# Row maxima over pairs of PSUM banks in six of sixteen attention units, and the transposed maxima in the scores' ring

## The reference

```python
xn = layernorm(x)                                   # x is (4, 512, 512)
q  = (xn @ wq).reshape(B, T, 32, 16)                # 32 heads of 16
k, v = xn @ wk, xn @ wv                             # one key and value head for all
scores = einsum('bqhd,bkd->bhqk', q, k) / 4
probs  = softmax(where(causal, scores, -inf))
s = einsum('bhqk,bkd->bqhd', probs, v).reshape(B, T, C) @ wo
g = silu(linear8bit(linear8bit(xn, W1, b1), W2, b2))  # rows rounded to int8 steps, outlier columns apart
out = x + s * g
```

## Time and profile before

| what | us |
|---|---|
| median of three runs | 789.14 |
| the three runs | 788.95, 789.14, 1225.57 |
| the profiled execution | 788.52 |
| its span, first to last instruction | 786.8 |
| attention, about | 82 to 400 |

### The profile page before, as it was taken

The page is one execution under the profiler, slowest core; times in us unless marked ns, Lnnn a source line. Parts: engine busy times, 40 slices in busy tenths (PEclk is TensorE's granted clock), DMA queues, the critical chain, the costliest instruction groups (busy, mean ns, idle before and its releaser), DMA issues. The chain is left out here.

```text
span 786.8 us, 11983 instructions
## 1 busy us (share of the span) xinstructions
PE 752.1 (96%) x4133; PEld 567.0 (72%) x4133; DVE 651.5 (83%) x1116; ACT 396.0 (50%) x671; POOL 273.6 (35%) x349
## 2 busy tenths in 40 slices
PE   5999899999999999999999999999997999999995
PEld 4877575556666677666568878878886888888884
DVE  7988989999989999987447668597859998599957
ACT  4454066676777677667824445355554333132212
POOL 7213135555555555555442112122100000027404
PEclk9999689999999999999999999999999999999998
DMA  7431302332333332233455677646334678427982
GB/s 261 157 108 54 78 21 70 86 83 76 91 91 105 89 83 84 83 83 122 135 192 185 166 237 197 202 105 161 88 62 131 240 241 255 157 87 245 332 278 107
DMA packets 93772, 110.71 MB, mean 141 GB/s; under 512 B 43136, under 2 KB 50320, under 8 KB 92176
## 3 DMA queue, kind: packets, MB, share of 16 engines
q1 hardware_dynamic: 93712, 109.95, 45.8%
HBM read 56.43 MB, written 40.37 MB: 123 GB/s over the span
## 5 line engine op out<-in xcount | busy, mean ns | idle before, releaser
L933 DVE TENSOR_REDUCE rowmax<-ps 128x2 f32<-128x512 f32 (+3 forms) x384 | 210.7, 590 | 20.3 <-PE ps L1010 18.7
L854 ACT ACTIVATE probs<-ps 128x512 f32<-128x512 f32 (+1 forms) x352 | 175.3, 557 | 72.0 <-PE ps L1023 70.3
L1010 PE MATMUL ps<-km,stack 128*128 128x256 f32 (+3 forms) x512 | 150.2, 347 | 2.6 <-PEq L195 1.9
L1023 PE MATMUL ps<-stack,ks 128*128 128x512 f32 (+1 forms) x352 | 132.8, 387 | 2.7 <-ACT probs L854 2.7
L1010 PEld LDWEIGHTS ps<-km,stack 128*128 128x128 f32 (+1 forms) x512 | 95.1, 199 | 43.1 <-DVE rowmax L933 23.5
L836 POOL TENSOR_SCALAR_AFFINE_SELECT probs<-probs 128x512 f32<-128x512 f32 x128 | 81.0, 641 | 78.9 <-ACT probs L854 77.3
L1880 PE MATMUL ps<-big_h 128*128 128x512 f32 x256 | 100.0, 390 | 2.0 <-DVE big_l L1696 1.6
L1881 PE MATMUL ps<-big_l,big_h 128*128 128x512 f32 x256 | 99.6, 389 | 0.0
L1882 PE MATMUL ps<-big_h,big_l 128*128 128x512 f32 x256 | 99.6, 389 | 0.0
L1036 PE MATMUL ps<-probs,vones 128*32 128x512 f32 (+3 forms) x1024 | 82.2, 439 | 0.2 <-POOL probs L836 0.2
L1023 PEld LDWEIGHTS ps<-stack,ks 128*128 128x128 f32 x352 | 67.4, 192 | 11.7 <-ACT probs L854 6.2
(11 more groups left out here) (227 smaller groups left out, 1370.0 us busy)
## 6 DMA issues: line engine op xcount, KB each, us to landing
stack<-big_h SPq DMA_DIRECT2D x128, 64.0 KB, 2.0
h_scratch<-hs SPq DMA_DIRECT2D x7, 1024.0 KB, 4.7
hload<-h_scratch SPq DMA_DIRECT2D x14, 512.0 KB, 5.2
xn_scratch<-xa SPq DMA_DIRECT2D x4, 1024.0 KB, 4.4
stack<-big_l SPq DMA_DIRECT2D x64, 64.0 KB, 2.0
xi<-xn_scratch SPq DMA_DIRECT2D x16, 256.0 KB, 2.7
xe_scratch<-xm SPq DMA_DIRECT2D x16, 256.0 KB, 2.3
w2n<-in_L_ffn_W_dram SPq DMA_DIRECT2D x4, 1024.0 KB, 6.5
```

What stands on the lines that cost most here:

```text
L854: nc.scalar.activation(probs[p][:, o:o + nh * w], ps[:, STB[n % NST], 0:nh * w], ACT.Exp).then_inc(s_exp, 1)
L933: nc.vector.tensor_reduce(dst, src, AX_X, ALU.max).then_inc(s_red, 1)
L1010: last = nc.tensor.matmul(dst, stack[u % 3][rows, hp, P * qt:P * (qt + 1)], km[rows, u // KT, p0:p0 + npar, keys], start=True, stop=True)
L1023: ins = nc.tensor.matmul(ps[:, STB[n % NST], 0:nh * w].rearrange("p (h q) -> p h q", h=nh), ks[:, u // KT, p, P * kt:P * (kt + 1)], stack[ ...
```

## The change

In units 0 to 5 (`PAIRED = KT + 2`) the pieces are taken in pairs. The order within a head pair is 4, 5, 1, 2, 0, 3. Two pieces that follow each other go to banks 0 and 1, the next two to banks 2 and 3. TensorE waits only ahead of the even piece, for the reduction of the pair before last, and tells VectorE only after the odd one. One reduction takes both banks: 768, 1024 and 768 columns. `rowmax` gets a row more, and its merge reads other rows. From unit 6 on, the pieces go through banks 0, 1 and 2 as before.

Bank 3 is then the projection's own. The scores' ring moves to banks 4, 5 and 6 and P·V to bank 7. The transposed maxima have no place in the projection's bank any more, in any unit: they take one turn in the scores' ring (`st_uses`), and who uses that bank next waits for `s_mh`. TensorE counts them in `s_mt`.

```diff
-        MAXB, STB, PVB, MISCB = (0, 1, 2), (3, 4, 5), 6, 7
+        MAXB, STB, PVB, MISCB = (0, 1, 2), (4, 5, 6), 7, 3
+        PAIRED = KT + 2
+        PAIR_ORDER = (4, 5, 1, 2, 0, 3)
+        def max_bank(u, c):
+            if u < PAIRED:
+                return 2 * ((CH * u + c) // 2 % 2) + c % 2
+            return MAXB[(CH * (u - PAIRED) + c) % NMAX]
+        def reduced(u, c):
+            if u < PAIRED:
+                return (CH * u + c) // 2 + 1
+            return CH * PAIRED // 2 + CH * (u - PAIRED) + c + 1
+        st_uses = []
+        for g in range(STEPS):
+            u, s_ = scored(g)
+            if 0 <= u < U and s_ < 2 * NB:
+                st_uses.append(("s", 2 * NB * u + s_))
+            if maximized(g, MAX_AT) >= 0:
+                st_uses.append(("m", maximized(g, MAX_AT)))
+        def st_free(engine, kind, i):
+            n = st_at[kind, i]
+            if n >= NST:
+                before, j = st_uses[n - NST]
+                engine.wait_ge({"s": s_exp, "m": s_mh}[before], j + 1)
...
@@ ScalarE, copy of the maxima
-                        n = misc_at[("m", u, 0)]
-                        act.wait_ge(s_mf, n + 1)
+                        act.wait_ge(s_mt, X_LOADED + u + 1)
...
-                        nc.scalar.copy(mhl[:, :], ps[0:2 * HPF, MISCB, :]).then_inc(s_mh, 1)
+                        nc.scalar.copy(mhl[:, :], st_bank("m", u)[0:2 * HPF, :]).then_inc(s_mh, 1)
...
@@ VectorE, reductions
-                        dve.wait_ge(s_max, g + 1)
...
+                        if u >= PAIRED or c % 2:
+                            dve.wait_ge(s_max, reduced(u, c))
...
+                                first = max_bank(u, c - 1)
+                                both = ps[:, first:first + 2, :]
+                                if m == 5:
+                                    src, dst = both[:, :, 0:P * (QT - 1)], mine[:, QT - 1, :, hp]
+                                elif m == 2:
+                                    src = both.rearrange("p s (a k) -> p s a k", a=2)
+                                    dst = mine[:, 1:QT - 1, :, hp]
+                                else:
+                                    src = both.rearrange("p s k -> p (s k)")[:, 2 * P:].rearrange(
+                                        "p (s a k) -> p s a k", s=3, a=2)
+                                    dst = mine[:, 0:2 * QT + 1:QT, :, hp]
...
@@ TensorE, max_piece, scores, misc_bank, maxima
-                    if n >= NMAX:
-                        pe.wait_ge(s_red, n - NMAX + 1)
-                    bank, o = ps[:, MAXB[n % NMAX], :], 0
+                    if u < PAIRED:
+                        if c % 2 == 0 and CH * u + c >= 4:
+                            pe.wait_ge(s_red, reduced(u, c) - 2)
+                    elif CH * (u - PAIRED) + c >= NMAX:
+                        pe.wait_ge(s_red, reduced(u, c) - NMAX)
+                    else:
+                        pe.wait_ge(s_red, CH * PAIRED // 2 - (c < 2))
+                    bank, o = ps[:, max_bank(u, c), :], 0
...
-                    last.then_inc(s_max, 1)
+                    if u >= PAIRED or c % 2:
+                        last.then_inc(s_max, 1)
...
-                    if n >= NST:
-                        pe.wait_ge(s_exp, n - NST + 1)
+                    st_free(pe, "s", n)
...
-                        kind, i, j = before[-1]
-                        if kind == "m":
-                            pe.wait_ge(s_mh, i + 1)
-                        else:
-                            pe.wait_ge(s_ob, QT * i + j + 1)
+                        _, i, j = before[-1]
+                        pe.wait_ge(s_ob, QT * i + j + 1)
+                    elif bank_of(use) == MISCB:
+                        pe.wait_ge(s_red, CH * PAIRED // 2)
...
-                    dst = misc_bank(("m", u, 0))
+                    st_free(pe, "m", u)
+                    dst = st_bank("m", u)
```

More of the change, by code:

```diff
@@ L125, in block_layernorm_attention_ffn @@
         later_k = sp_("later_k", [P, P])
-        s_x0 = [sem(f"x_tile{j}_loaded_then_w1_rows") for j in range(QT)]
+        s_x0 = [sem(f"x_tile{j}_loaded_then_later_stage") for j in range(QT)]
         X_LOADED = 16
@@ L694, in block_layernorm_attention_ffn, with st_bank @@
         misc_at = {use: n for n, use in enumerate(misc)}
+        st_uses = []
[5 more added lines that the diff above has]
+                st_uses.append(("m", maximized(g, MAX_AT)))
+        st_at = {use: n for n, use in enumerate(st_uses)}
+        def st_bank(kind, i):
+            return ps[:, STB[st_at[kind, i] % NST], :]
+        def st_free(engine, kind, i):
[3 more added lines that the diff above has]
+                engine.wait_ge({"s": s_exp, "m": s_mh}[before], j + 1)
         def bank_of(use):
@@ L919, in _ @@
                         u, c = divmod(g, CH)
-                        hp, m = divmod(c, 6)
+                        hp, m = piece_of(u, c)
+                        mine = rowmax[:, u % 2, :, :].rearrange("p s (a h) -> p s a h", a=2)
                         if c == 0 and u >= 2:
-                            dve.wait_ge(s_mf, misc_at[("m", u - 2, 0)] + 1)
-                        dve.wait_ge(s_max, g + 1)
[L924 to L927, removed]
-                        else:
[L929 to L932, removed]
@@ L933, in _ @@
-                        nc.vector.tensor_reduce(dst, src, AX_X, ALU.max).then_inc(s_red, 1)
+                            dve.wait_ge(s_mt, X_LOADED + u - 1)
+                        if u >= PAIRED or c % 2:
+                            dve.wait_ge(s_max, reduced(u, c))
+                            bank = max_bank(u, c)
+                            if u < PAIRED:
[10 more added lines that the diff above has]
+                                    dst = mine[:, 0:2 * QT + 1:QT, :, hp]
+                            elif m == 3:
+                                src = ps[:, bank, :].rearrange("p (s a k) -> p s a k", s=2, a=2)
+                                dst = mine[:, QT:2 * QT + 1:QT, :, hp]
+                            else:
+                                qt, _, p0, npar = PIECES[m][0]
+                                w = P * (qt + 1) if qt < 2 else P * qt
+                                src = ps[:, bank, 0:npar * w].rearrange("p (a k) -> p a k", a=npar)
+                                dst = mine[:, qt, p0:p0 + npar, hp]
+                            nc.vector.tensor_reduce(dst, src, AX_X, ALU.max).then_inc(s_red, 1)
@@ L934, in _ @@
                         if c == CH - 1:
-                            dve.wait_ge(s_red, g + 1)
-                            nc.vector.tensor_tensor(mine[:, 2:QT, :], mine[:, 2:QT, :], mine[:, QT:QT + 2, :],
+                            dve.wait_ge(s_red, reduced(u, c))
+                            whole = rowmax[:, u % 2, 2:QT, :]
+                            nc.vector.tensor_tensor(whole, whole, rowmax[:, u % 2, QT:2 * QT + 1:QT, :],
                                                     ALU.max).then_inc(s_rm, 1)
@@ L1020, in scores @@
                         pe.wait_ge(s_sm[u % 3], 16 * (u // 3 + 1))
-                    if n >= NST:
-                        pe.wait_ge(s_exp, n - NST + 1)
-                    ins = nc.tensor.matmul(ps[:, STB[n % NST], 0:nh * w].rearrange("p (h q) -> p h q", h=nh),
+                    st_free(pe, "s", n)
+                    ins = nc.tensor.matmul(st_bank("s", n)[:, 0:nh * w].rearrange("p (h q) -> p h q", h=nh),
                                            ks[:, u // KT, p, P * kt:P * (kt + 1)],
@@ L1073, in maxima @@
                                                    ident[:, :])
-                    last.then_inc(s_mf, 1)
+                    last.then_inc(s_mt, 1)
                 for g in range(STEPS):
```

25 lines of the change are left out of this document (15 added, 10 removed).

## The result

The changed kernel takes 798.64 us (median of 4 runs, 797.12 to 801.07) against 789.05 before: a ratio of 1.012 with a 95% interval of 1.0099 to 1.014. One of the four executions of the kernel before took 1225.57 us and is left out of the ratio. The profiled execution took 799.14 us.

What follows compares the result with a forecast made beforehand. VectorE was taken to bound units up to 5, TensorE those from 6 on. Terms of +1.2, +1.7, +0.9, +6.5 and -1.0 summed to +9.3 us, giving 798 us, range 786 to 804 (the forecast's own: 793 to 802).

Steps and rivals of the forecast that it cites:

- Fewer reductions, 0.06 us each: Units 0 to 5: 12 fewer VectorE reductions a unit, 0.06 us each, saving 0.7 us a unit, 4.3 in all.
- The ring, late units: Units 6 to 15: the score after piece 6 waits for ScalarE's copy of the maxima; 0.65 us net each, +6.5 us.
- Units 2 to 5, +0.3 each: Coarser hand-over costs 1.0 us a unit, fewer reductions save 0.7; +0.3 us each, +1.2 us for four units.
- the stall costs nothing: Units 2 to 5: VectorE has a transpose to do while the score waits for the copy, so no cost there.
- The three places in the pairs' ledger: Three spots in each of units 2 to 5 where pairs delay VectorE: +0.40, +0.3 and +0.3 us, together 1.0.
- step 22: Pair (22, 23) has a P·V run between its pieces, leaving 768 columns to reduce instead of 384: +0.40 us.
- step 14: Transpose of the second P·V result waits for a P·V run, uncovering about half a 512-column reduction: +0.3 us.
- steps 4 and 5: TensorE comes late to this pair, and VectorE has only one 1.13 us reduction to bridge it: +0.3 us.
- Unit 0, +1.7; unit 1, +0.9: At half clock, filling pairs outlasts VectorE's cover, stalling 0.8 us a head pair; net +1.7 and +0.9 us.
- The tail, -1.0: At the end, the projection no longer waits 1.04 us on TensorE for the last maxima: -1.0 us.
- The first rival: Either the reductions' saving holds and the copy's stall costs, about 790 us, or the reverse, about 791; chance 0.25.
- The third rival: Granted clock stays at 1.2 GHz through unit 2, which takes about 26 us instead of 17.5; 807 us, chance 0.10.

Runs made afterwards that it cites:

- experiment 3: Changed kernel with ScalarE's copy of the transposed maxima moved ahead of the exponential of step 4: 789.75 us, ratio 1.0016 to before; run again, 789.11 us.
- experiments 3 and 4: The second of these: the changed kernel with the early copy of experiment 3 and no pairs in any unit: 786.92 us, ratio 0.9983 to before.
- experiment 1: Changed kernel without pairs in any unit, the transposed maxima keeping their turn in the scores' ring: 796.99 us, ratio 1.011 to before.
- experiment 5: Experiment 3 with two of a unit's four P·V runs moved one step later, so none stands inside a pair: 787.58 us, ratio 0.9972 to before.
- experiment 10: The changed kernel run once more, unchanged, for its profile: 798.0 us.
- experiment 7: Kernel before with only ScalarE's copy of the maxima moved ahead of the exponential, maxima in the projection's bank: 786.63 us, ratio 0.9971.

## Why the prediction was right

The time (798 for 798.64) and the largest cost, with its mechanism, were right. That the total came so near is in part luck: against the sum of +9.3, the terms were off by -1.0 (unit 0), -0.6 (unit 1), +0.8 (units 2 to 5), +0.6 (the ring in late units), +1.3 (the tail) and +0.24 (the start of unit 0, which had no term), and these cancel to +1.3. The profiled execution is 10.6 us longer than that of before, the medians differ by 9.6. Step by step, by the profiled execution:

- **Fewer reductions, 0.06 us each.** Right: 0.87 and 1.13 us, as worked out, for 768 and 1024 columns. By these numbers crossing a bank costs nothing. VectorE's busy time fell from 16.90 to 16.41 us a unit, by 0.5 where I had 0.7 (by 0.6 in experiment 3, 16.28).
- **The ring, late units.** Right: 0.72 us of delay in unit 10, as forecast, 0.71 net a unit where I took 0.65; +7.08 for +6.5. Experiment 3 removes the cause and with it the cost.
- **Units 2 to 5, +0.3 each.** Too small (0.44 in units 3 to 5, 0.68 in unit 2), and the account of it did not hold. The pairs, freed of the ring's stall, cost 0.14 a unit in units 3 to 5 and 0.42 in unit 2 (experiments 3 and 4), and the stall adds 0.34 to them (17.63 to 17.97). The step that failed is "the stall costs nothing" there: it costs 0.6 without pairs (experiment 1). I looked for cover at the place of the stall, and not at the long run behind it.
- **The three places in the pairs' ledger.** At step 22 VectorE's 0.64 us of idle time and the longer reduction behind it are there (+0.40 to the merge, as forecast, and +0.11 of idle time); experiment 5, which moves that run out of the pair, removes the wait. At step 14 the transpose waits 0.13 us, not 0.3. At steps 4 and 5 nothing waits. In their place VectorE waits 0.20 us at 155.89, behind the P·V run that the ring's stall delays (no such wait is booked in experiment 3), and 0.32 us at 162.78 for GpSimd's division of the P·V result, which I had not looked for.
- **Unit 0, +1.7; unit 1, +0.9.** Too large: +0.70 and +0.30. Over all profiles unit 0 takes 13.83 to 13.88 us with pairs and 13.15 to 13.36 with single pieces in three banks, so the pairs cost 0.5 to 0.7 there. The mis-sized term is the pair of 1024 columns. In the third head pair the reductions start at 89.78, 90.80 and 91.94, the next head pair's first at 93.18. Less the reductions' own 0.87, 1.13 and 0.87, the stalls are 0.15 us ahead of the pair (1,2), 0.01 ahead of (0,3) and 0.37 ahead of (4,5): 0.5 in all. I had 0.50, 0.02 and 0.29, 0.8 in all. The 1024 columns are there 1.02 us behind the pair before them, where I took 1.28: of the 0.44 that I added to their 0.85 us, 0.17 is there. Unit 1 is blurred by the clock's own variation.
- **The tail, -1.0.** The wait of 1.04 us on the maxima is gone, but the tail as a whole is 0.3 us longer. TensorE's waits behind unit 15 (total, times, longest), where before it waited for the same DMA once, for 0.7 us:

```profile
PE ps L1157 <- DMA tail_rows<-xe_scratch: 1.4, 3, 0.8
PE ps L1120 <- ACT projected_rows L755: 0.5, 1, 0.5
```

  The last of these transposes starts 24.6 us behind the last merge before, and 24.6 in the changed kernel. It is 23.9 in experiment 10, the same kernel, and 23.5 in experiment 1, but 24.6 again in experiment 7, where the wait on the maxima is gone, too. So the wait is gone, and a later wait for rows of a DMA took the time in this execution. That any time is gained is not shown: the same kernel differs from itself by 0.7 us there.

The first rival (one half of the change costs, the other doesn't) had both its halves tested apart, and both cost. The third rival (the clock stays low through unit 2) is seen in none of the 13 profiled executions: the granted clock is 1.00 at the latest from 108 us on. Of the executions without a profile only the mean clock is known. The slowest of the changed kernel, 801.07 us, had 0.977 where the others had 0.985 to 0.989; so a clock that stays low for longer may be in it, but it cost about 2 us, not the 9 of that rival.

## What to carry to other kernels

When a buffer joins a ring, look at what frees it and where that instruction stands in its engine's queue. Here a copy one place too late cost 8.5 us in units 2 to 15, of 9.6 us in the whole, and exchanging it with the exponential gave them back. A stall that something covers on the spot must still be followed to the next long run on its engine, which it delays. With the runs where they stood, a spare bank was worth more as depth (17.20 us a unit) than as width (17.63): coarser hand-over saves instructions, and pays for them wherever other work stands between the halves. With that work moved out of the pairs, width came to the same 17.2.

## What I had not expected of the hardware

- A VectorE reduction over two PSUM banks takes its columns and one start: 1.13 us for 1024 columns where two of 512 take 1.20. I had left room for a price of the bank's edge.
- The half clock in units 0 and 1 lasted 13.65 us in one profile of experiment 3, and 17.1 us, in two stretches, in the other. The Trainium skill ("TensorE: Matmul & The Clock Gate", Part 1) says that the slow start of one and the same kernel varies between runs. That is said of a kernel's start; here the half clock begins 82 to 86 us into the span, and the two profiles show that its length varies there as well, with 14.79 and 16.23 us for unit 1.
